# Scatter of a step's last turn behind the second layer, maximum parts ahead of the first turn's scatter, early fetches one unit later: a fused attention and routed feed-forward kernel on one Trainium2 core

## The chip, the cores and the metric

One core of a Trainium2 chip runs the whole program in one launch. The metric is device time in microseconds (us). The core has TensorE (PE, matrix products), VectorE (DVE), ScalarE (ACT), GpSimd (POOL) and SyncE (SP, which only issues transfers here). Each engine works through its own queue in order and waits on semaphores. GpSimd issues indirect transfers: gathers and scatters of rows by a list of indices.

## What is computed

`x` has 16 batches of 256 tokens with 128 features. The rows are normalised. From them come two things: causal attention with 16 heads of 8 features (low-rank corrections to the weights, a linear position bias), and a feed-forward network of 8 experts, of which each token uses one.

```python
xn = _layernorm(x, axis=-1)
s = _L0_attn_ref(xn, ...)            # softmax(q k^T / sqrt(8) + alibi + mask) v, then Wp
# experts:
indices = jnp.argmax(softmax(xn @ Wr + br), axis=-1)
for i in range(8):
    mask = (indices == i)[..., None]
    h = relu((xn * mask) @ W1[i] + b1[i])
    out = out + (h @ W2[i] + b2[i])
g = _silu(out)
return x + s * g
```

## The kernel before

**Steps and turns.** The attention runs as `NB` = 16 steps, one batch each. A step `i` has `NG` = 6 turns `g` = 0 to 5 (`GROUPS`, line 81). A turn has two units of scores (the last has one); a unit is a set of head pairs of one block row. For a unit TensorE makes the scores of step `i` (lines 1246 and 1254) and, beside them, the scores of step `i + 2` from which only the row maxima are taken (lines 1226 and 1234, read by VectorE at line 807). ScalarE turns the scores into probabilities (line 746). The products with the values come in bursts (line 1298): the last burst of a step stands in turn 0 of the next.

**Maximum parts.** The row maxima of a batch are split by GpSimd into three bf16 parts, five small instructions (`max_parts`, lines 552 to 560). TensorE transposes them at turn 2 (`turn_max`, line 1309), ScalarE copies them out (line 650), and SyncE stores them into the stack of queries at turn 3 (`load_max_rows`, line 416). The scores of the next step wait for that store. GpSimd makes the parts of batch `i + 1` at turn 0 of step `i`.

**Experts.** The tokens are sorted by expert into `SLOT_TILES` = 39 tiles of 128 rows. GpSimd gathers the rows of a tile from DRAM (`fetch_rows`, line 519), TensorE transposes four tiles at a time (line 1340), applies the first layer (`hidden`, line 1348) and the second (`output`, line 1356). VectorE applies relu (line 1030) and moves the result into one of three buffers `y_slot` (`keep_y`, line 1036); GpSimd scatters it to the rows of the tokens in DRAM (`scatter_y`, line 533). `TURNS` gives each tile a turn: tiles 0 to 3 stand at turns 21 to 24, counted over all steps, the others at `g` = 2, 3, 5 and 0. At a tile's turn TensorE makes first its first layer, then the second layer of the tile before it. The scatter of tile `t` stands at `SCATTER_TURNS[t]`: turns 23, 24, then every turn with `g` = 2, 3, 5 or 0 to turn 78, which holds two. There tile `t + 2` has its first layer. Fetches stand at `FETCH_AT`: tiles 0 to 11 one a turn from (2, 4) to (4, 3), the others at `g` = 4, 5, 1 and 2.

**Order on GpSimd.** The loop at lines 583 to 600 writes it out by hand: in each turn the fetches, at `g` = 3 the third part of a batch four steps ahead (line 506), the scatters, at `g` = 0 the maximum parts. In front of a fetch or a scatter stands a wait for a bank that TensorE filled, which sets when in the turn GpSimd issues it.

**SyncE.** At turn 0 it stores zeros and the first parts of queries and keys of batch `i + 3` (lines 405, 411, 373, 379), at turn 1 the second parts. From turn 80, that is (13, 2), it loads the experts' rows back in eight transfers (`load_y`, line 449); the first waits until all scatters have landed.

**End.** ScalarE applies tanh (line 710), VectorE multiplies and adds (lines 1042, 1048, 1053), SyncE stores.

Of the kernel before, what the change touches and what calls it, by code (L numbers as in the profile page):

```python
# [33 lines left out]
NB, T, D = 16, 256, 128  # L34
# [63 lines left out]
TILES_AT = {place: (t,) for t, place in enumerate(PLACES)}  # L98
# [107 lines left out]
def program(nc, x, w_dense, lora, br, b1, w_experts, const_f32, const_bf16, const_rows, zero_rows, out):  # L206
# [14 lines left out]
    with ctx:  # L221
# [129 lines left out]
        def wait_vec_full(eng, *key):  # L351
            k, use = VEC[key]
            eng.wait_ge(vec_full[k], use + 1)
            return vec_bank[k], vec_empty[k]

        def wait_act_full(eng, *key):
            k, use = ACTS[key]
            eng.wait_ge(act_full[k], use + 1)
            return act_bank[k], act_empty[k]

        def wait_vec_emptied(eng, *key):
            k, use = VEC[key]
            eng.wait_ge(vec_empty[k], use + 1)
# [130 lines left out]
        def _(pool):  # L494
# [7 lines left out]
            def third_part(b):  # L502
                r = b % PART_BUFS
                wait(pool, f"q3_out{r}", 16 * COPIES[2] * (b // PART_BUFS))
                pool.wait_ge(S["part2_done"], b + 1)
                pool.tensor_tensor(parts[:, r, 2], rem[:, b % 2], parts[:, r, 1], ALU.subtract).then_inc(S["part3_done"], 1)  # L506
# [4 lines left out]
            def fetch_rows(t):  # L511

                q = t // 4
                if t == 0:
                    pool.wait_ge(S["rows_done"], 1)
                    pool.wait_ge(S["rows_kept"], 16 * 4)
                if q >= 2:
                    wait_act_full(pool, "rows", q - 2)
                pool.indirect_dma_start(xs_slot[:, q % 2, t % 4, :], None, xn_dram[:, :],  # L519
                                        bass.IndirectOffsetOnAxis(from_row[:, t:t + 1], axis=0)).then_inc(S[f"xs_in{t % 8}"], 16)  # L520

            def tile_numbers():

                pool.wait_ge(S["tile_place_done"], 1)
                pool.tensor_tensor(tile_hot[:, :, 1, :], tile_hot[:, :, 1, :], tile_ids.unsqueeze(2).to_broadcast([P, NT, SLOT_ROWS]),
                                   ALU.mult).then_inc(S["tile_hot_done"], 1)

            def scatter_y(t):

                wait_vec_emptied(pool, "y", t)  # L530
                if t == 0:
                    pool.wait_ge(S["tokens_done"], 1)
                pool.indirect_dma_start(y_dram[:, :], bass.IndirectOffsetOnAxis(token_of[:, t:t + 1], axis=0),  # L533
                                        y_slot[:, t % 3, :], None).then_inc(S[f"y_out{t % 3}"], 16)
# [11 lines left out]
            def max_parts(b):  # L546

                r = b % 2
                for u in range(NU):
                    wait_vec_emptied(pool, "max", b, u)  # L550
                wait_act_full(pool, "nmax", b - 2)
                pool.tensor_scalar(nmax[r][:, :, 0, :], row_max[r][:, :, :], -1.0, None, ALU.mult).then_inc(S["nmax1"], 1)
                pool.wait_ge(S["nmax1"], b + 1)
                pool.tensor_tensor(nmax_rem[:, :, :], row_max[r][:, :, :], nmax[r][:, :, 0, :], ALU.add).then_inc(S["nmax_r"], 1)
                pool.wait_ge(S["nmax_r"], b + 1)
                pool.tensor_scalar(nmax[r][:, :, 1, :], nmax_rem[:, :, :], -1.0, None, ALU.mult).then_inc(S["nmax2"], 1)
                pool.wait_ge(S["nmax2"], b + 1)
                pool.tensor_tensor(nmax_rem2[:, :, :], nmax_rem[:, :, :], nmax[r][:, :, 1, :], ALU.add).then_inc(S["nmax_r2"], 1)
                pool.wait_ge(S["nmax_r2"], b - 1)
                pool.tensor_scalar(nmax[r][:, :, 2, :], nmax_rem2[:, :, :], -1.0, None, ALU.mult).then_inc(S["nmax3"], 1)  # L560
# [22 lines left out]
            for i in range(NB):  # L583
                for g, units in enumerate(GROUPS):
                    for t in FETCH_AT.get((i, g), ()):
                        wait_act_full(pool, "scores", i, units[0])
                        fetch_rows(t)
                    if g == PROJECT + 2 and i + AHEAD < NB:
                        third_part(i + AHEAD)
                    for t in range(SLOT_TILES):  # L590
                        if SCATTER_TURNS[t] == i * NG + g:
                            if g in (0, 3):
                                wait_act_full(pool, "scores", i, units[1])
                            elif TILES_AT[i, g][0] < SLOT_TILES:
                                wait_vec_full(pool, "hidden", TILES_AT[i, g][0])
                            scatter_y(t)
                    if g == 0 and 0 < i < NB - 1:
                        max_parts(i + 1)
                    if (i, g) == TILE_HOT_AT:
                        tile_numbers()  # L600

# [940 lines left out]
```

## Time and profile before

| | us |
|---|---|
| median of 3 runs | 317.42 |
| lowest and highest | 315.58, 317.52 |
| the profiled execution | 316.19 |
| its span, first to last instruction | 314.3 |
| busy in it: TensorE | 291.0 |
| VectorE | 214.8 |
| ScalarE | 206.6 |
| GpSimd | 132.8 |

The granted clock of TensorE is 0.986 of full on average. GpSimd issues 39 gathers and 39 scatters. The profiled execution is 1.23 us below the median of the runs. The chain of work that ended last goes for 76% of the span through TensorE. The release "issue" in a row means that the engine waited for nothing that the profile shows.

### The profile page before, as it was taken

To read this page: it belongs to the slowest core of one execution; us is meant where nothing else is said; L and a number is where in the kernel's file an instruction comes from. 1 tells how busy PE (TensorE), PEld (TensorE's weight loads), DVE (VectorE), ACT (ScalarE), POOL (GpSimd) and SP (SyncE) were. 2 spreads that over 40 slices of the span, in tenths; PEclk is the share of its full clock that TensorE was granted. 3 is DMA by queue.
4 is the path that set the end of the run, shared out by engine and by line. 5 is a ranking of instruction groups with operands and counts; after the bars stand their busy time and mean duration, and the time that the engine had idled before them with its cause. 6 is when DMAs were issued, how large, how long until landed. Compare 5 with 4: busy or idle time off the path is not lost.

```text
span 314.3 us, 13158 instructions
## 1 busy us (share of the span) xinstructions
PE 291.0 (93%) x5330; PEld 221.9 (71%) x5330; DVE 214.8 (68%) x480; ACT 206.6 (66%) x379; POOL 132.8 (42%) x210
## 2 busy tenths in 40 slices
PE   8899989898979899999999999999999998989893
PEld 3467468575657778878787787878878786867652
DVE  4788996899955475665657566575756656574893
ACT  2343265645568487777787777787777866669981
POOL 3065271122354646655645565564656422241000
PEclk9999999999979999999999999999999999999996
DMA  4799499643141311414223142231414222008432
GB/s 136 211 235 206 123 292 339 162 134 93 28 118 48 108 52 49 116 49 116 57 64 86 50 114 58 80 83 37 116 51 103 67 53 79 20 29 240 141 99 71
DMA packets 46811, 33.89 MB, mean 108 GB/s; under 512 B 5048, under 2 KB 44216, under 8 KB 46624
## 3 DMA queue, kind: packets, MB, share of 16 engines
q1 hardware_dynamic: 42520, 26.80, 31.8%
q0 software_dynamic: 2496, 5.12, 6.1%
q10 hardware_dynamic: 1736, 1.14, 1.5%
q8 instruction: 43, 0.70, 1.0%
q14 instruction: 16, 0.13, 0.1%
HBM read 13.17 MB, written 6.75 MB: 63 GB/s over the span
## 4 chain that ended last, share of the span: by engine, by line
PE 76%; DVE 11%; issue 4%; ACT 4%; DMA 2%; SPq 1%; POOL 0%; ACTq 0%; DVEq 0%; POOLq 0%
PE bank L1348 13%; PE bank L1298 12%; PE bank L1246 11%; PE bank L1356 11%; PE bank L1254 5%; DVE row_max L807 4%; PE bank L1159 4%; PE bank L1332 3%; PE bank L1166 3%; PE bank L1318 2%; DVE w_slots L972 2%; ACT probs L746 2%; PE bank L1226 2%; PE bank L1175 2%; PE bank L1340 2%
## 5 line engine op out<-in xcount | busy, mean ns | idle before, releaser
L807 DVE TENSOR_REDUCE row_max<-bank 128x2 f32<-128x512 f32 (+3 forms) x176 | 106.9, 637 | 31.8 <-PE bank L1234 29.1
L746 ACT ACTIVATE probs<-bank 128x512 f32<-128x512 f32 (+1 forms) x176 | 90.1, 560 | 33.9 <-PE bank L1254 31.7
L1246 PE MATMUL bank<-qk_stack 64*64 64x64 bf16 (+3 forms) x1024 | 60.9, 236 | 3.4 <-DVE row_max L807 1.5
L1226 PE MATMUL bank<-qk_stack 64*64 64x64 bf16 (+3 forms) x1024 | 61.4, 236 | 0.8 <-DMA qk_stack<-parts 0.5
L519 POOL DMA_INDIRECT xs_slot<-normalised_rows,from_row x39 | 38.4, 985 | 47.1 <-PE bank L1254 41.4
L533 POOL DMA_INDIRECT expert_rows<-y_slot,token_of x39 | 38.6, 991 | 46.1 <-PE bank L1348 32.8
L1030 DVE TENSOR_TENSOR hT<-bank,w_slots 128x512 f32<-128x512 f32 x39 | 27.0, 692 | 35.5 <-PE bank L1348 34.8
L722 ACT ACTIVATE w_slots<-w_all 128x1156 f32 x39 | 45.6, 1169 | 4.5 <-issue 3.2
L1246 PEld LDWEIGHTS bank<-qk_stack 64*64 64x64 bf16 x1024 | 34.1, 107 | 20.0 <-issue 8.5
L1298 PE MATMUL bank<-probs,v_diag 128*32 128x64 f32 (+3 forms) x1024 | 45.9, 304 | 1.2 <-issue 1.0
L1348 PE MATMUL bank<-xsT_slot,w_slots 128*128 128x128 f32 x312 | 45.3, 285 | 1.5 <-issue 1.5
L1254 PE MATMUL bank<-cb 64*64 64x128 bf16 (+2 forms) x352 | 43.3, 241 | 0.0
L1234 PE MATMUL bank<-cb 64*64 64x128 bf16 (+2 forms) x352 | 43.2, 241 | 0.0
L1356 PE MATMUL bank<-w_slots,hT 128*128 128x128 f32 x312 | 42.0, 276 | 0.2
L1348 PEld LDWEIGHTS bank<-xsT_slot,w_slots 128*128 128x128 f32 x312 | 38.1, 191 | 3.9 <-issue 1.8
L1356 PEld LDWEIGHTS bank<-w_slots,hT 128*128 128x128 f32 x312 | 38.2, 192 | 1.5 <-issue 1.4
L1226 PEld LDWEIGHTS bank<-qk_stack 64*64 64x64 bf16 x1024 | 33.7, 107 | 5.9 <-issue 4.7
L1298 PEld LDWEIGHTS bank<-probs,v_diag 128*32 128x32 f32 x1024 | 25.1, 109 | 12.4 <-issue 1.7
L506 POOL TENSOR_TENSOR parts<-rem,parts 128x512 bf16<-128x512 f32 x15 | 17.5, 1164 | 20.1 <-ACT parts L634 19.9
L1133 PE MATMUL bank<-zeros 128*128 128x512 bf16 x60 | 18.8, 420 | 2.3 <-POOL zeros L496 1.0
L641 ACT ACTIVATE v_diag<-bank 64x256 f32<-64x256 f32 x32 | 12.1, 379 | 12.9 <-PE bank L1166 11.8
L1254 PEld LDWEIGHTS bank<-cb 64*64 64x64 bf16 x352 | 19.8, 108 | 0.0
(134 smaller groups left out, 379.0 us busy)
## 6 DMA issues: line engine op xcount, KB each, us to landing
qk_stack<-parts SPq DMA_DIRECT2D x120, 64.0 KB
qk_stack<-parts SPq DMA_DIRECT2D x32, 128.0 KB
w_all<-w_experts SPq DMA_DIRECT2D x8, 512.0 KB, 5.9
normalised_rows<-xn_all SPq DMA_DIRECT2D x4, 512.0 KB, 6.9
xn_all<-expert_rows SPq DMA_DIRECT2D x8, 256.0 KB, 4.9
out<-xn_all SPq DMA_DIRECT2D x7, 256.0 KB, 2.5
x_all<-x SPq DMA_DIRECT2D x3, 512.0 KB, 5.2
xs_slot<-normalised_rows,from_row POOLq DMA_INDIRECT x39
```

What stands on the lines that cost most here:

```text
L519: pool.indirect_dma_start(xs_slot[:, q % 2, t % 4, :], None, xn_dram[:, :], bass.IndirectOffsetOnAxis(from_row[:, t:t + 1], axis=0)).then_ ...
L533: pool.indirect_dma_start(y_dram[:, :], bass.IndirectOffsetOnAxis(token_of[:, t:t + 1], axis=0), y_slot[:, t % 3, :], None).then_inc(S[f"y ...
L722: act.activation(w_slot[t % 3], w_all[:, bass.ds(e, 1), :].rearrange("p o f -> p (o f)"), ACT.Copy).then_inc(S["w_done"], 1)
L746: act.activation(probs[:, m % PROBS, 0:w], bank[:, 0:w], ACT.Exp).then_inc(emptied, 1)
L807: dve.tensor_reduce(row_max[b % 2][:, n, pairs[0]:pairs[-1] + 1], bank[:, 0:ln_u * len(pairs)].rearrange("p (c k) -> p c k", k=ln_u), AX.X ...
L1226: pe.matmul(bank[to, c * ln_u:(c + 1) * ln_u], q[rows, p, n * BLK:(n + 1) * BLK], k[rows, p, 0:(n + 1) * BLK], start=(c == 0), stop=False, ...
L1234: last = pe.matmul(bank[to, 0:ln_u * len(pairs)].rearrange("p (c k) -> p c k", k=ln_u)[:, :, n * BLK:], ident_b[rows, rows], mask_qk[rows] ...
L1246: pe.matmul(bank[rows, c * ln_u:(c + 1) * ln_u], k[rows, p, kb * BLK:(kb + 1) * BLK], q[rows, p, kb * BLK:], start=(c == 0), stop=False, s ...
L1254: last = pe.matmul(bank[rows, 0:ln_u * len(pairs)].rearrange("p (c k) -> p c k", k=ln_u)[:, :, 0:BLK], ident_b[rows, rows], mask_kq[rows]. ...
L1298: last = pe.matmul(pv_bank[32 * j:32 * j + 32, half * T + kb * BLK:(half + 1) * T], v_diag[b % 2][:, kb, p, :], probs[:, (b * NU + w) % PR ...
L1348: last = pe.matmul(bank[:, c * P:(c + 1) * P], w_slot[t % 3][:, c * P:(c + 1) * P], xsT_slot[:, t // 4 % 2, t % 4, :], start=(c == 0), sto ...
L1356: last = pe.matmul(bank[:, 0:D], hT[:, t % 2, c, :], w_slot[t % 3][:, W2 + c * D:W2 + (c + 1) * D], start=(c == 0), stop=(c == NC_H - 1))
```

## The change

In GpSimd's loop, and nowhere else:

- A fetch at `g` = 0 (tiles 2 and 8) waits for the scores of the turn's second unit instead of the first.
- `max_parts` stands ahead of the turn's scatters instead of behind them.
- A scatter at `g` = 5 waits until the second layer of the tile before the turn's tile is in its bank, instead of the first layer of the turn's tile.

```diff
             for i in range(NB):
                 for g, units in enumerate(GROUPS):
                     for t in FETCH_AT.get((i, g), ()):
-                        wait_act_full(pool, "scores", i, units[0])
+                        wait_act_full(pool, "scores", i, units[-1] if g == 0 else units[0])
                         fetch_rows(t)
+                    if g == 0 and 0 < i < NB - 1:
+                        max_parts(i + 1)
                     if g == PROJECT + 2 and i + AHEAD < NB:
                         third_part(i + AHEAD)
                     for t in range(SLOT_TILES):
                         if SCATTER_TURNS[t] == i * NG + g:
                             if g in (0, 3):
                                 wait_act_full(pool, "scores", i, units[1])
+                            elif g == 5:
+                                wait_vec_full(pool, "y", TILES_AT[i, g][0] - 1)
                             elif TILES_AT[i, g][0] < SLOT_TILES:
                                 wait_vec_full(pool, "hidden", TILES_AT[i, g][0])
                             scatter_y(t)
-                    if g == 0 and 0 < i < NB - 1:
-                        max_parts(i + 1)
```

## Rows read from the trace of the kernel before

**Rows 1.** The page: busy time, share of the span and instructions of each engine.

```profile
PE 291.0 (93%) x5330; PEld 221.9 (71%) x5330; DVE 214.8 (68%) x480; ACT 206.6 (66%) x379; POOL 132.8 (42%) x210
```

**Rows 2.** Stretches of steps 7 and 11: length, busy per engine, clock, transfers.

```profile
149.70:168.95 19.25, 18.49 (x343) 15.13 (x343) 11.92 (x23) 14.44 (x26) 10.48 (x15) 1.00 0.28 74
...
224.74:243.21 18.47, 18.06 (x343) 14.98 (x343) 11.82 (x23) 14.16 (x26) 10.56 (x15) 1.00 0.31 73
```

**Rows 3.** Chain of waits, first turns of steps 4, 7 and 10: start, us, what.

```profile
106.92 0.75 PE bank L1348 x5
...
111.74 0.87 PE bank L1159 x4
...
164.91 0.53 PE bank L1348 x3
...
168.95 0.86 PE bank L1159 x4
...
221.50 1.09 PE bank L1348 x8
...
224.74 0.86 PE bank L1159 x4
```

**Rows 4.** Timeline of TensorE: start, us, instruction, idle before and its releaser.

```profile
108.92 0.27 PE L1348 MATMUL bank<-xsT_slot,w_slots 128*128 128x128 f32 x1 [0.58 <-issue]
...
166.20 0.59 PE L1348 MATMUL bank<-xsT_slot,w_slots 128*128 128x128 f32 x3 [0.33 <-issue]
```

**Rows 5.** Timeline of GpSimd from step 6's last turn into step 7.

```profile
162.80 1.00 POOL L533 DMA_INDIRECT expert_rows<-y_slot,token_of  x1 [0.53 <-PE bank L1348]
164.73 0.98 POOL L533 DMA_INDIRECT expert_rows<-y_slot,token_of  x1 [0.94 <-PE bank L1254]
165.74 0.33 POOL L552 TENSOR_SCALAR nmax<-row_max 128x32 bf16<-128x32 f32 x1
...
167.18 0.29 POOL L560 TENSOR_SCALAR nmax<-nmax_rem 128x32 bf16<-128x32 f32 x1
168.36 1.05 POOL L519 DMA_INDIRECT xs_slot<-normalised_rows,from_row  x1 [0.89 <-PE bank L1254]
```

**Rows 6.** Chain of waits, the second layer in that last turn.

```profile
162.51 0.89 PE bank L1356 x8
```

**Rows 7.** Timeline of GpSimd from step 3's last turn into step 4.

```profile
104.64 1.00 POOL L533 DMA_INDIRECT expert_rows<-y_slot,token_of  x1 [0.30 <-issue]
106.59 0.98 POOL L519 DMA_INDIRECT xs_slot<-normalised_rows,from_row  x1 [0.95 <-PE bank L1254]
107.87 1.00 POOL L533 DMA_INDIRECT expert_rows<-y_slot,token_of  x1 [0.30 <-issue]
```

**Rows 8.** Timeline from step 12's last turn to the start of step 14.

```profile
274.34 0.96 POOL L533 DMA_INDIRECT expert_rows<-y_slot,token_of  x1 [6.10 <-PE bank L1348]
...
278.60 0.96 POOL L533 DMA_INDIRECT expert_rows<-y_slot,token_of  x1 [1.61 <-DVE y_slot L1036]
...
281.02 0.29 POOL L560 TENSOR_SCALAR nmax<-nmax_rem 128x32 bf16<-128x32 f32 x1
281.36 0.29 PE L1309 MATMUL bank<-cb,nmax 128*32 128x64 bf16 x8 [1.02 <-POOL nmax L560]
...
282.14 0.38 SPq L449 DMA_DIRECT2D xn_all<-expert_rows  x1
282.56 0.62 SPq L416 DMA_DIRECT2D qk_stack<-nmaxT  x1
...
286.04 0.41 PE L1246 MATMUL bank<-qk_stack 64*64 64x256 bf16 x4
```

**Rows 9.** The page, transfer queues: packets, MB, share of 16 engines' span.

```profile
q8 instruction: 43, 0.70, 1.0%
```

**Rows 10.** Transfers by line: count, KB each, median us to landing.

```profile
out<-xn_all SPq DMA_DIRECT2D x2, 128.0 KB, 1.8
```

## The prediction

> **What bounds the kernel now.** I read the page's busy shares first. TensorE is busy 291.0 of 314.3 us and the next engine 214.8 [rows 1], so a change that only moves GpSimd's work can give back no more than TensorE's idle time, some 23 us with start and end, or stretched time of the matmuls themselves. Then the stretches by step: a step of the middle takes 18.4 to 19.3 us, with TensorE busy 18.06 of 18.47 in a short one and 18.49 of 19.25 in a long one [rows 2]. So the steps are bound by TensorE, yet equal work differs by 0.8 us. To find where, I read the chain of waits at the first turn of a step, from the start of a tile's first layer (line 1348) to the start of the projection (line 1159). That stretch holds the same instructions in every step. It lasts 3.24 us in step 10 (221.50 to 224.74; steps 5 and 11 come within 0.04 of it), but 4.04 in step 7 (164.91 to 168.95) and 4.82 in step 4 (106.92 to 111.74) [rows 3]. The same two rows of step 6 give 3.77, those of steps 8 and 9 give 3.50 each. Over 3.24 that is 0.53 + 0.80 + 0.26 + 0.26 = 1.85 us for steps 6 to 9, and 1.58 us for step 4. The timeline shows what the excess is: TensorE stops in the middle of the eight matmuls of one tile, where the kernel has no wait, with "issue" as the releaser [rows 4]. A last place stands apart: in step 13 TensorE waits 1.02 us for the maximum parts of GpSimd (line 560) [rows 8]. In steps 4 to 12 GpSimd releases TensorE nowhere.
>
> **The change, part by part.**
>
> **1. Scatter at g == 5 waits for `y` instead of `hidden`** (10 places, (3, 5) to (12, 5)). It adds and removes no instruction. In step 7 the scatter starts at 162.80 and the second layer at 162.51, where the first ended, so it follows its releaser by some 0.3 us [rows 5, 6]. The second layer takes 0.89 in the chain [rows 6], so it ends at 163.40 and the scatter starts at about 163.7 instead of 162.80: 0.9 us later, ending 164.7. Behind it on GpSimd stands what the first turn of the next step brings. The buffer it empties is wanted two tiles later (`keep_y` of tile t + 3, at g == 2, about 173.5), ten microseconds on, so by itself this costs nothing; if that cover were gone, each microsecond of delay would come back on VectorE, then on the bank that it empties.
>
> **2. Maximum parts ahead of the scatter at g == 0.** The five parts run from 165.74 to 167.47, 1.73 us [rows 5]. Started when part 1's scatter ends, they run from about 164.7 to 166.45. Their inputs are there: the step's last maxima come at the end of the turn before, and the parts never waited for them here. The scatter behind them waits for the second unit's scores as before, which have been full since before 164.73, and runs from 166.6 to 167.6 instead of 164.73 to 165.71. It is the queue item that gets later, by 1.9 us; its buffer is wanted at g == 3, eight microseconds on. Next in GpSimd's queue is the fetch at (i, 1), at 168.36 [rows 5]: still free to start on time, but now only a fraction of a microsecond behind a scatter instead of behind the parts. The fetched rows are wanted many turns later. Priced as waits, parts 1 and 2 are worth 0 in steps 5 to 12.
>
> **3. Early fetches.** Only the fetches at g == 0 are touched, tiles 2 and 8. That of tile 2 stands in a queue that runs behind after the row numbers come late, and both units of its turn are scored before the transfer ahead of it ends, so I give it 0. That of tile 8 starts at 106.59 and moves by the length of one unit, some 0.3 us. More matters the scatter behind it: 107.87, 0.30 us after the fetch ended [rows 7]. After the change the 1.73 us of parts stand between these two, so it starts near 110; nothing is taken off the path by that unless the stop of part 4 goes with it.
>
> **4. What the stops cost.** No row prices a stop against the place of an indirect transfer, so I bound it from both sides. The stops in the middle of a tile's or a burst's matmuls in steps 3 to 9 all lie in the first turn, in which SyncE's six to seven stores to the stacks meet GpSimd's transfers; TensorE's 0.58 us stop of step 4 ends at 108.92, right behind the end of the second of two transfers standing 0.30 us apart (107.87 + 1.00) [rows 4, 7]. In step 7 the 0.33 us stop comes just after the one at 164.73 [rows 4, 5]. With the scatter of the first turn moved 2 us back and the fetch-scatter pair of step 4 opened, step 4 may lose its 1.58 us and steps 6 to 9 their 1.85 us: that is the gain's end, -3.4. The other end is nothing, or the stops of the rival below. For step 4, whose pair is really taken apart, I take -0.9, a little over half; for steps 6 to 9, where the same transfers still fall into the same crowd, -0.5, about a quarter, since three steps with the same order (5, 10, 11) show none [rows 3].
>
> The chip's instruction stream crosses the same engines: queue 8 moved 43 packets and 0.70 MB in the run, some 16 KB each [rows 9]. The Trainium skill (Runtime: NRT & Kernel Launch, Instruction fetch mechanics) says that instructions are refilled in 16 KiB blocks and that this is hidden, because the sequencer dispatches slower than the refill. The packet size agrees; the stops inside one tile's matmuls [rows 4] speak against "hidden", but no row names their cause. By that rule the stops would have nothing to do with transfers and part 4 would be 0 instead of -1.4; this is the second rival.
>
> **5. Step 13.** The scatter of (12, 5) starts at 274.34 and would start at about 275.2 (0.9 us later, as in part 1), ending 276.2. The parts then run from 276.2 to 277.95, 3.4 us ahead of their end at 281.31 now, and the 1.02 us wait at 281.36 goes [rows 8]. What is late next? Both scatters of (13, 0) come behind the parts: the first at about 278.1, the last, 0.96 + 0.30 us on, at 279.4 instead of 278.60: 0.8 us later. SyncE's first load of the expert rows (line 449) waits for it: now 282.14, which would be 282.9. Behind that in the same queue stands the load of the maximum rows (line 416), now 282.56, then 283.4, and TensorE needs it for step 14, now at 286.04, wanted at 285.02 if the 1.02 us is kept [rows 8]. Its time to landing is at least about the 1.8 us of the output's 128 KB stores [rows 10], and at most 3.48 (286.04 less 282.56), since TensorE does not wait there now. So TensorE would wait between 0.2 and 1.8 us, and this step is worth from -0.8 to +0.8. I take 2.3 us, nearer to the lone small store than to a landing in a crowd: it lands at 285.7, and -0.4 is left. That the row is fetched a step ahead in all other steps is why this matters only here.
>
> **Sum:** -0.9 - 0.5 - 0.4 = -1.8 us against the profiled execution, whose 316.19 us are the span of 314.3 and 1.9 around it: 314.4. The median of the three runs, 317.42, lies 1.2 above that execution (their lowest, 315.58, lies 0.6 below it), so against the median I say 315.6.
>
> **Rivals.**
>
> **All stops go** (chance 0.2). What ends them is the distance between GpSimd's transfers and the thick of the stores. For it: every stop lies there. Against it: steps 5, 10 and 11. It would give 3.4 us and another 0.4 to 0.8 from step 13, so -4.0: 313.4.
>
> **Nothing of the stops changes** (0.24). SyncE's stores alone, or the refill by itself, make them, and the scatter is one of eight or so transfers of the turn. The Trainium skill (Trainium Kernel Development and Optimization, Key Constraints) puts SP's, ACT's and POOL's transfers on the same 16 engines, where they interleave; by it a scatter moved by 2 us inside the same crowd is no relief. Only step 13 is left, -0.4: 317.0.
>
> **A new pair in every step** (0.11, the slower side). The scatter of (i, 0) ends at 167.6 and the fetch of (i, 1) follows: 0.3 to 0.7 us between two indirect transfers in steps 4 to 11, eight times, where 1.73 us of parts stood before. If closeness of two such transfers is what stops TensorE, at 0.5 to 0.8 us each (step 6's and 7's excess), eight pairs cost 4.0 to 6.4, less what step 4 gets back: about +3.5, 321. Against it: the scatter at 104.64 stands 0.30 us behind a fetch too, with no stop beside it [rows 7], and by 168 us SyncE has issued all stores of the turn. It decides from some six pairs that stop for 0.5 us.
>
> **The wait at g == 5 does not bite** because GpSimd arrives late anyway: here it is idle 0.53 us ahead of 162.80 [rows 5], so the new wait does move it; I fold the few hundredths of chance for it into the second rival.
>
> **How the numbers follow.** The forecast case has 0.45, the rivals 0.20, 0.24 and 0.11. Own range of the forecast case: 314.3 to 317.2, from the ends of step 13 and half the ends of part 4. The whole range goes down to the middle of the first rival and up past the second with the runs' own spread: 313.2 to 318.4, leaving out the slower rival and the far end of the first. 1% is 3.2 us, about what can be told from no change. Faster by more: the first rival's 0.20 less a little, and the lower edge of the forecast's, 0.27. Slower by more: 0.11 of the last rival, rounded to 0.12. Within: 0.61.
>
> **What would show it.** Part 1: the scatter of a g == 5 turn starts 0.8 to 1.0 us later within its step, behind line 1356. Part 2: the five parts end near the place where they began, the scatter behind them, no `keep_y` idle. Part 4: the stretch from line 1348 to line 1159 at the first turn is near 3.3 us in step 4 and in steps 6 to 9; if it stays at 3.5 to 4.0 there, I was wrong to credit it, and if it grows in steps 5, 10 and 11 the pairs are guilty. Part 5: line 1309 of step 13 no longer waits for line 560, while line 449 starts 0.8 us later and TensorE may show a wait on a transfer at the start of step 14. The prediction falls if the total moves by over 3 us either way.

## The result and the profile after

The changed kernel took 317.57 us (median of 22 runs) against 315.81 us (22 runs) of the kernel before in the same comparison. The ratio is 1.0055, 95% interval 1.0036 to 1.0075: a small loss, about 1.7 us, where I had forecast a small gain. Later sets of runs, told of below, gave two kinds of answer: some in which the kernel before takes about 305 us and the change gains 0.2 to 0.3%, and some in which it takes about 316. The sets at about 305 ran on chips 12, 0, 0 and 4, the later set at about 316 on chip 8; for the first comparison no chip is on record. Whether the difference goes with the chip or with something else about a set is not known: no chip gave both answers.

The page after has the same busy time of TensorE in a longer span (compare [rows 1]):

```profile
span 315.6 us, 13158 instructions
...
PE 291.1 (92%) x5330; PEld 221.9 (70%) x5330; DVE 216.2 (68%) x480; ACT 206.6 (65%) x379; POOL 133.0 (42%) x210
```

Step 11 as a stretch, from turn 1 to turn 1 (columns as in [rows 2]); it takes 19.17 us where the kernel before had 18.47 in [rows 2]. This stretch goes from line 1320 to line 1320, the start of turn 1, that of [rows 2] from line 1159 to line 1159; both span one whole step:

```profile
224.68:243.85 19.17, 18.29 (x350) 15.15 (x343) 11.93 (x22) 14.23 (x24) 10.46 (x14) 1.00 0.30 72
```

Lines of the changed kernel from 600 on are two higher: 1350 is the first layer, 1300 the burst of products with the values. The chain of waits in the first turn of step 10 shows where the time went. It answers to the last two rows of [rows 3]. In the kernel before the burst ahead of them took 0.82 us:

```profile
220.68 0.82 PE bank L1298 x32
```

In the changed kernel:

```profile
220.80 0.68 PE bank L1300 x22
221.48 0.21 issue
221.69 0.40 PE bank L1300 x9
222.09 1.09 PE bank L1350 x8
223.18 0.89 PE bank L1358 x8
...
224.75 0.59 PE bank L1320 x4
225.34 0.86 PE bank L1161 x4
```

From line 1350 to line 1161 it is now 3.25 us, clean, as it was at best before. The eight long matmuls of a tile no longer stop. The burst of 32 short matmuls ahead of them does: 0.68 + 0.21 + 0.40 = 1.29 us. Of the 0.47 us more only 0.21 shows as idle. The timeline of step 8 (the same in steps 5 to 13) sets it beside GpSimd:

```profile
182.23 0.99 POOL L533 DMA_INDIRECT expert_rows<-y_slot,token_of  x1 [1.42 <-PE bank L1358]
182.55 0.75 PE L1300 MATMUL bank<-probs,v_diag 128*32 128x128 f32 x23
183.26 0.33 POOL L552 TENSOR_SCALAR nmax<-row_max 128x32 bf16<-128x32 f32 x1
183.56 0.40 PE L1300 MATMUL bank<-probs,v_diag 128*32 128x64 f32 x9 [0.26 <-issue]
```

The scatter's preparation on GpSimd ends at 183.22; TensorE is idle from 183.30. In all nine steps 5 to 13 the distance from that end to the stop lies between 0.07 and 0.12 us. The new wait ties the scatter to the end of the second layer, so its end falls into the burst each time. I call that end the launch of the transfer.

Step 13 answers to [rows 8]:

```profile
280.01 1.03 POOL L533 DMA_INDIRECT expert_rows<-y_slot,token_of  x1 [0.39 <-issue]
281.35 0.97 POOL L533 DMA_INDIRECT expert_rows<-y_slot,token_of  x1 [0.31 <-issue]
281.49 2.12 PE L1300 MATMUL bank<-probs,v_diag 128*32 128x256 f32 x16
283.27 0.30 PE L1311 MATMUL bank<-cb,nmax 128*32 128x64 bf16 x8
283.66 0.38 SPq L449 DMA_DIRECT2D xn_all<-expert_rows  x1
284.21 0.62 SPq L416 DMA_DIRECT2D qk_stack<-nmaxT  x1
```

Line 1311 waits no more for the parts. But the two scatters that now follow the parts, 0.31 us apart, run over the burst of 16 at (13, 1), which takes 2.12 us. In the kernel before it took 1.07:

```profile
279.27 1.07 PE L1298 MATMUL bank<-probs,v_diag 128*32 128x256 f32 x16
```

The 1.02 us won is spent again. One launch alone did not stretch this burst before: the last scatter of [rows 8] ends at 279.56, 0.3 us into it, and TensorE does not stop. The same holds for the bursts of 16 matmuls at turn 1 of steps 3 and 4 of the changed kernel, with launches at 93.65 and 112.16. So a launch inside a burst is not enough by itself for a stop; what sets the burst of 32 apart is not known.

### The profile page after: what moved, and what is told of

The parts are those of the page before. It is cut to its first block, busy times and chain, and to the rows that moved or that the text cites. A ratio compares the mean times of both kernels' runs of the same rounds, so it can differ in the third digit from the quotient of the medians.

```text
span 315.6 us, 13158 instructions
## 1 busy us (share of the span) xinstructions
PE 291.1 (92%) x5330; PEld 221.9 (70%) x5330; DVE 216.2 (68%) x480; ACT 206.6 (65%) x379; POOL 133.0 (42%) x210
## 4 chain that ended last, share of the span: by engine, by line
PE 75%; DVE 12%; ACT 4%; issue 4%; DMA 2%; SPq 1%; DVEq 1%; ACTq 0%
PE bank L1350 13%; PE bank L1300 12%; PE bank L1248 12%; PE bank L1358 11%; PE bank L1256 5%; DVE row_max L809 5%; PE bank L1334 3%; PE bank L1161 3%; PE bank L1168 3%; PE bank L1320 2%; DVE w_slots L974 2%; PE bank L1228 2%; ACT probs L748 2%; PE bank L1177 2%; PE bank L1342 2%
## 5 line engine op out<-in xcount | busy, mean ns | idle before, releaser
L809 DVE TENSOR_REDUCE row_max<-bank 128x2 f32<-128x512 f32 (+3 forms) x176 | 108.0, 637 | 38.5 <-PE bank L1236 33.5
L748 ACT ACTIVATE probs<-bank 128x512 f32<-128x512 f32 (+1 forms) x176 | 91.1, 560 | 44.4 <-PE bank L1256 39.0
L1300 PE MATMUL bank<-probs,v_diag 128*32 128x64 f32 (+3 forms) x1024 | 49.3, 305 | 3.1 <-issue 2.8
L1248 PEld LDWEIGHTS bank<-qk_stack 64*64 64x64 bf16 x1024 | 33.9, 106 | 20.7 <-issue 8.7
L1350 PE MATMUL bank<-xsT_slot,w_slots 128*128 128x128 f32 x312 | 44.3, 285 | 0.0
L1358 PE MATMUL bank<-w_slots,hT 128*128 128x128 f32 x312 | 41.3, 275 | 0.0
L1300 PEld LDWEIGHTS bank<-probs,v_diag 128*32 128x32 f32 x1024 | 26.8, 109 | 15.8 <-issue 5.7
L1228 PEld LDWEIGHTS bank<-qk_stack 64*64 64x64 bf16 x1024 | 33.2, 106 | 6.2 <-issue 5.0
L506 POOL TENSOR_TENSOR parts<-rem,parts 128x512 bf16<-128x512 f32 x15 | 17.5, 1166 | 20.2 <-ACT parts L636 19.9
L1256 PEld LDWEIGHTS bank<-cb 64*64 64x64 bf16 x352 | 19.7, 107 | 0.0
L1236 PEld LDWEIGHTS bank<-cb 64*64 64x64 bf16 x352 | 19.6, 107 | 0.0
```

The lines of the kernel that those rows point to most:

```text
L748: act.activation(probs[:, m % PROBS, 0:w], bank[:, 0:w], ACT.Exp).then_inc(emptied, 1)
L809: dve.tensor_reduce(row_max[b % 2][:, n, pairs[0]:pairs[-1] + 1], bank[:, 0:ln_u * len(pairs)].rearrange("p (c k) -> p c k", k=ln_u), AX.X ...
L1228: pe.matmul(bank[to, c * ln_u:(c + 1) * ln_u], q[rows, p, n * BLK:(n + 1) * BLK], k[rows, p, 0:(n + 1) * BLK], start=(c == 0), stop=False, ...
L1236: last = pe.matmul(bank[to, 0:ln_u * len(pairs)].rearrange("p (c k) -> p c k", k=ln_u)[:, :, n * BLK:], ident_b[rows, rows], mask_qk[rows] ...
L1248: pe.matmul(bank[rows, c * ln_u:(c + 1) * ln_u], k[rows, p, kb * BLK:(kb + 1) * BLK], q[rows, p, kb * BLK:], start=(c == 0), stop=False, s ...
L1256: last = pe.matmul(bank[rows, 0:ln_u * len(pairs)].rearrange("p (c k) -> p c k", k=ln_u)[:, :, 0:BLK], ident_b[rows, rows], mask_kq[rows]. ...
```

## The experiments

Each experiment was timed against the kernel before on the same chip. Ratios have their 95% interval.

### Parts alone

The first set: the new wait alone; the maximum parts alone; the change without the new wait; and the change with a later wait.

```diff
# the wait alone: the kernel before with
+                            elif g == 5:
+                                wait_vec_full(pool, "y", TILES_AT[i, g][0] - 1)
# the parts alone: max_parts(i + 1) moved ahead of the scatters
# the later wait: the changed kernel with
-                                wait_vec_full(pool, "y", TILES_AT[i, g][0] - 1)
+                                pool.wait_ge(S["pv_ps"], (i + 1) * NPV)
```

> The kernel before with the new wait of the scatters at g = 5 alone. Theory A (every pause of TensorE begins some 0.1 us after GpSimd has finished preparing an indirect transfer, and the new wait puts that moment into the burst of short matmuls at line 1298): a stop of about 0.2 us in that burst in each of the ten steps, the burst 1.3 us long instead of 0.82, so the whole slowdown of the change or more is here, ratio to before 1.006 to 1.012 (the early gain of step 4 and of part 2 missing). Theory B (the new neighbourhood of the first turn's scatter and the fetch behind it makes the loss): no change here, 0.998 to 1.002.

> The kernel before with the maximum parts ahead of the first turn's scatter, nothing else. Theory A: the scatter of g = 5 keeps its place, so the burst at line 1298 stays at 0.82 us; the first turn's scatter now finishes beside the second layer, the scores of the next turn or the transposition at line 1318, and the stops of steps 4 and 6 to 9 in line 1348 go: ratio 0.985 to 0.997, with line 1309 of step 13 no longer waiting. Theory B: the loss is here, ratio 1.003 to 1.010.

> The changed kernel with the wait at g = 5 put back (maximum parts first, early fetches one unit later). Theory A: like maximum parts first alone, 0.985 to 0.997 of before, that is 1 to 2% below the changed kernel. Theory B: 1.003 to 1.010 of before, the changed kernel's own time.

> The changed kernel with the scatters of g = 5 made to wait still longer, until the burst at line 1298 of the next step's first turn is done. Theory A: what hurts is the moment, not the lateness; the end of the preparation leaves the burst and falls about 1.3 us behind it, into the long matmuls of lines 1350 and 1358: burst back to 0.82 us, ratio to before 0.990 to 1.001. Theory B (a later scatter pushes the whole queue of GpSimd and its transfers into the next turn): worse than the changed kernel, 1.008 or more.

The kernel before took 305.2 us here, with the instructions as long as in the first trace. The wait alone: 0.9994 (0.9975 to 1.0013). The parts alone: 0.9970 (0.9939 to 1.0002). The change without the wait: 0.9983 (0.9959 to 1.0008). The later wait: 1.0060 (1.0037 to 1.0082). Theory A's loss for the wait did not come, for there was no stop in any burst. So the set could not judge it. The later wait lost by something else: in step 13 everything behind the burst is late, and the maximum rows with it.

```profile
277.29 0.41 PE L1248 MATMUL bank<-qk_stack 64*64 64x256 bf16 x4 [1.87 <-DMA qk_stack<-nmaxT]
```

### The change itself in such a set

Unaltered kernels, and the wait alone again.

> The changed kernel unaltered, beside the kernel before on the same chip. In the first comparison the kernel before took 315.8 us and TensorE stopped for 0.2 to 0.6 us about 0.1 us after indirect transfers were prepared; in the single-part runs it took 305.2 and no such stop was seen. Theory A (the loss is made of these stops): where there are none the change is not slower, ratio 0.996 to 1.001; where they are back, 1.003 to 1.008. Theory B (the loss comes from the order of the waits and is there on any chip): 1.004 to 1.008 in either case.

> The kernel before unaltered, one look, for its trace on the chip of this set. Theory A: if it takes about 305 us, steps 6 to 12 are 18.1 us each with no stop in lines 1298 or 1348; if it takes about 316, the stops of the first trace are there again.

> The new wait at g = 5 alone once more, on the chip of this set. Theory A: where the kernel before takes about 316 us, a stop in the burst at line 1298 of each step and a ratio of 1.004 to 1.012; where it takes about 305, 0.998 to 1.002 as before. Theory B: the same ratio on both.

The kernel before: 305.4 us median. The changed kernel: 0.9973 (0.9961 to 0.9986), the wait alone 1.0011 (0.9996 to 1.0027). So the change is faster where the stops are missing, and its steps 6 to 11 are 18.06 or 18.07 us from turn 1 to turn 1, as those of the kernel before. In the changed kernel the scatter of step 8 runs from 176.07 to 177.06, inside the burst, and the chain has the burst whole:

```profile
176.07 0.99 POOL L533 DMA_INDIRECT expert_rows<-y_slot,token_of  x1 [1.42 <-PE bank L1358]
```

```profile
176.46 0.80 PE bank L1300 x32
177.26 0.31 PE bank L1350
```

The 0.27% is step 13. The kernel before waits there as in [rows 8], the changed kernel waits for the maximum rows a little later instead:

```profile
271.00 0.29 PE L1309 MATMUL bank<-cb,nmax 128*32 128x64 bf16 x7 [1.02 <-POOL nmax L560]
```

```profile
275.16 0.38 PE L1248 MATMUL bank<-qk_stack 64*64 64x256 bf16 x3 [0.45 <-DMA qk_stack<-nmaxT]
```

From turn 1 of step 13 to turn 1 of step 14 it is 9.51 us instead of 10.23: 0.72 less.

### The dose, and the parts where launches pause TensorE

This set had the kernel before at 316.5 us. First an extra gather of 128 rows at each g = 5, ten in all, whose data is not used; the same with a plain transfer; the kernel before with the maximum parts first in step 13 only and the first load of expert rows behind the maximum rows; and the parts alone.

```diff
# the dose: the kernel before with, behind the scatter of g == 5,
+                                wait_vec_full(pool, "y", TILES_AT[i, g][0] - 1)
+                                wait(pool, "probe_in", 16 * (i - 3))
+                                pool.indirect_dma_start(probe[:, :], None, xn_dram[:, :], ...from_row[:, 0:1]...)
# or, plain:
+                                pool.dma_start(probe[:, :], xn_dram[0:P, :])
```

> The kernel before with one more gather of 128 rows into a spare tile at each g = 5, launched when the changed kernel launches its scatter there; its data is not used. Theory A on a chip where launches pause TensorE (kernel before about 316): a stop of 0.2 to 0.3 us in the burst at line 1298 of every step 4 to 13, 3 to 6 us more, ratio 1.010 to 1.020. On a chip without pauses (about 305): 0.999 to 1.002, for transfers and their preparation are hidden. Theory C (what pauses is the instruction refill behind a crowd of transfers): stops not bound to the place, in some steps only.

> As the gather before, but a plain transfer of the same 64 KB issued by GpSimd, its data not used either. If the pause belongs to indirect transfers alone: ratio of the gather kernel not reached, 0.999 to 1.003 on both kinds of chip. If it belongs to any transfer that GpSimd prepares: like the gather.

> The kernel before with maximum parts first in step 13 alone, and SyncE's first load of expert rows put behind the load of the maximum rows; scatters and fetches elsewhere as before. Both theories: the 1.02 us wait at line 1309 goes, and the wait on the maximum rows at the start of step 14 that the changed kernel had instead (0.45 us) does not come: 0.9 to 1.3 us less than before, ratio 0.996 to 0.998, on a chip with pauses and on one without.

> Maximum parts first alone once more. On a chip without pauses 0.996 to 0.998 as measured. On a chip with pauses, theory A: the burst at line 1298 stays whole, so at least as good as on the other, 0.990 to 0.999; theory B: the scatter of the first turn and the fetch behind it make the loss, 1.003 to 1.008.

The dose: 1.0426 (1.0383 to 1.0470), 329.06 us, or 1.26 us for each gather, two to four times what I expected. Here line 1304 is the burst, 602 the extra gather; scatter and gather end at 188.20 and 189.46:

```profile
187.20 1.00 POOL L535 DMA_INDIRECT expert_rows<-y_slot,token_of  x1 [0.53 <-PE bank L1354]
188.50 0.96 POOL L602 DMA_INDIRECT probe<-normalised_rows,from_row  x1 [0.31 <-issue]
```

```profile
189.40 0.34 PE L1304 MATMUL bank<-probs,v_diag 128*32 128x64 f32 x4 [0.32 <-issue]
190.36 0.43 PE L1304 MATMUL bank<-probs,v_diag 128*32 128x64 f32 x12 [0.62 <-issue]
```

TensorE stops twice in the burst: at 189.09, 0.9 us behind the end of the scatter and while the gather is still being prepared, and at 189.74, 0.28 us behind the gather's end. The first keeps no such short distance to an end as the nine of the changed kernel do. In seven of the eight steps 5 to 12 it lies over packets of the scatter itself, which in step 8 begin to move at 188.93; in the changed kernel no packet of GpSimd's transfers is under way during any of the nine stops (in step 8 they begin at 183.89, behind it). So the dose shows what the gathers cost, and not that each stop is set by the end of a preparation; the moving data may have a share in its first stops. Its bursts in steps 4 to 13 all hold stops (in step 13, at 288, only one). Bound to the place and there in each step, they speak for the indirect transfers and against a refill of instructions that would come at other points of each step. The packets of queue 8 in the trace of the changed kernel say the same: the nearest to the nine stops begin between 2.0 us ahead of them and 2.7 us behind, and in seven of the nine stops none is under way.

The plain transfer: 1.0031 (0.9999 to 1.0063), hardly anything. Its ten preparations all end inside the burst, 0.3 to 0.6 us behind the burst's start, and none of the ten bursts has a stop. In step 8 the end is at 182.91 (TensorE's row is from the chain of waits):

```profile
182.32 0.59 POOL L602 DMA_DIRECT2D probe<-normalised_rows  x1
```

```profile
182.60 0.84 PE bank L1304 x31
```

So of the two readings, every transfer of GpSimd or the indirect ones alone, this speaks for the second. It is not clean: the plain preparation is shorter, 0.59 us against 0.96 to 1.00, and ends 0.3 us into the burst, where that of the gather ended 1.0 us after the burst had begun and that of the changed kernel's scatter 0.7 us.

The parts alone: 0.9907 (0.9882 to 0.9931), 3.4 us faster than the kernel before. The step in its chain, lines as before:

```profile
218.74 0.82 PE bank L1298 x32
219.57 1.09 PE bank L1348 x8
220.66 0.89 PE bank L1356 x8
222.22 0.59 PE bank L1318 x4
222.81 0.87 PE bank L1159 x4
```

and GpSimd beside it:

```profile
217.46 0.99 POOL L533 DMA_INDIRECT expert_rows<-y_slot,token_of  x1 [0.53 <-PE bank L1348]
218.48 0.33 POOL L552 TENSOR_SCALAR nmax<-row_max 128x32 bf16<-128x32 f32 x1
...
220.63 1.05 POOL L533 DMA_INDIRECT expert_rows<-y_slot,token_of  x1 [0.41 <-issue]
222.37 0.99 POOL L519 DMA_INDIRECT xs_slot<-normalised_rows,from_row  x1 [0.69 <-PE bank L1254]
```

The launches fall at 218.45 (in the scores, 0.3 us ahead of the burst), 221.68 (behind the second layer) and 223.36 (in the projection): none in the burst, none in the first layer. All steps from 6 to 11 last 18.44 to 18.53 us, where the kernel before had 18.44 to 19.25 in its first trace. One stop of 0.36 us in the first layer is left, in step 4. This kernel has the close pair of scatter and fetch too, 0.69 us apart where the changed kernel has 0.54, so that pair is not what costs; theory B falls.

The last-step kernel: 1.0003 (0.9973 to 1.0032), no gain where 0.2 to 0.4% was expected. Its wait at the transposition is gone as well (line 1313 there), and again two scatters, 0.30 us apart, stand beside the burst of (13, 1), lines four higher:

```profile
277.43 1.03 POOL L535 DMA_INDIRECT expert_rows<-y_slot,token_of  x1 [0.39 <-issue]
278.77 0.97 POOL L535 DMA_INDIRECT expert_rows<-y_slot,token_of  x1 [0.30 <-issue]
```

```profile
279.66 1.40 PE L1302 MATMUL bank<-probs,v_diag 128*32 128x256 f32 x13
```

Step 13 takes 9.98 us there from turn 1 to turn 1, where the kernel before had 10.25 in its first trace.

### The wait alone beside the change, twice more, and the best version

> The changed kernel in one set with its parts. Theory A on a chip with pauses (kernel before about 316): 1.003 to 1.008, the stop in the burst in every step. On a chip without (about 305): 0.996 to 0.999. Theory B, without part 1 being guilty: no link to the burst's stops.

> The new wait at g = 5 alone. Theory A on a chip with pauses: the stop in the burst of every step, and 1.005 to 1.020, since what the maximum parts in front bring (0.991 alone there) is missing. If part 1 hurts only together with part 2 (two scatters shifted by the same 1 to 2 us): 0.997 to 1.003. On a chip without pauses: 1.000.

> The changed kernel with the g = 5 scatters held until the burst is done. Theory A (place in the burst) on a chip with pauses: burst whole again at 0.80 us, 0.993 to 1.001 of before, below the changed kernel. If lateness or crowding of launches is what counts, not the burst: 1.005 to 1.015. On a chip without pauses it took 1.006, from waits of its own.

> Maximum parts first in all steps, and SyncE's first load of expert rows behind the load of the maximum rows; no new wait, no fetch change. With pauses 0.988 to 0.993, without 0.995 to 0.997: the best of all in both cases if the two gains add.

> The changed kernel beside its parts. Theory A where the kernel before takes about 316: 1.003 to 1.008 with the stop in the burst of every step; where it takes about 305: 0.996 to 0.999.

> The new wait at g = 5 alone. Theory A where the kernel before takes about 316: a stop in the burst of every step, 1.005 to 1.020. If the wait hurts only with the maximum parts moved too: 0.997 to 1.003. About 305: 1.000.

> The changed kernel with the g = 5 scatters held until the burst is done. Theory A where the kernel before takes about 316: burst whole at 0.80 us, 0.993 to 1.001. If lateness of launches counts and not the burst: 1.005 to 1.015. About 305: 1.006 to 1.008 as measured.

Both sets had the kernel before at 305.4 to 305.6 us, so neither could show the stops. The changed kernel: 0.9981 (0.9964 to 0.9998) and 0.9966 (0.9952 to 0.9979). The wait alone: 1.0007 (0.9977 to 1.0038) and 1.0015 (1.0003 to 1.0027). The later wait: 1.0078 (1.0056 to 1.0101) and 1.0056 (1.0037 to 1.0075). Maximum parts first in all steps, with the first load of expert rows put behind the maximum rows on SyncE, was the best of its set: 0.9971 (0.9959 to 0.9983).

```diff
-                    if (i, g) in LOAD_AT:
+                    if (i, g) in LOAD_AT and LOAD_AT[i, g] > 0:
+                        if LOAD_AT[i, g] == 1:
+                            load_y(0)
                         load_y(LOAD_AT[i, g])
```

Its step 13 takes 9.02 us from turn 1 to turn 1, 1.2 less than before; the parts alone in their first set, without that order, had 9.02 too. So the order of the loads gave nothing that was measured. The parts alone are the version to take: 0.991 in the one kind of set, 0.997 in the other.

## Why the prediction was wrong

**What bounds.** Right: the steps are TensorE's, and the spread between equal steps is stops in the middle of its matmuls. I even had the rows side by side in part 4, a stop of 0.58 us that ends behind a launch and one of 0.33 that begins 0.16 us behind another [rows 4, 5, 7].

**Part 1 is the step that failed.** I moved the scatter at g = 5 by 0.9 us (measured: it starts 1.42 us after the fetch ahead of it instead of 0.53, 0.89 later) and priced that at nothing in steps 5 to 12, because I asked only who waits for the buffer. I did not carry the launch that comes 1 us behind the start against TensorE's own sequence. 163.7 + 1.0 is 164.7, and the burst of step 7 began at 164.08 and lasted 0.83. The price was 0.45 to 0.60 us in each burst of steps 6 to 12, by the chain of waits. A second cost stood behind it: the wait for ScalarE ahead of the values' projection at turn 3 (line 1166, now 1168) grew from about 0.40 us to between 0.47 and 0.71 us per step; it was 4.1 us instead of 2.8 over steps 5 to 11. For that second one I have only the trace; which launch makes ScalarE late was not isolated.

**Part 4** was half right. The stops in the first layer did go, all 1.85 us of steps 6 to 9, not the quarter that I took. Others came in the burst. The two go apart: the kernel with the parts alone lost the first in steps 5 to 12 and did not gain the second. From turn 1 of step 5 to turn 1 of step 12 the sum was: bursts +3.5, first layer -1.85, turn 3 +1.3, together +3.0; measured 133.81 us against 130.71, so +3.1. Ahead of that the changed kernel had gained 1.00 us: its turn 1 of step 5 begins at 129.11 instead of 130.11. Step 4 took 18.75 us from turn 1 to turn 1 instead of 20.91, which is 2.2 less and not the 0.9 I had put there, but step 5 took 0.77 more, and 0.42 had been lost ahead of turn 1 of step 2. Behind turn 1 of step 12 the changed kernel is 0.84 us shorter, of which 0.76 stands behind the last matmuls of line 1320; I have no cause for that. -1.00 + 3.10 - 0.84 is the +1.26 of the two spans. Not all of step 4's gain is the change: the kernel before had a granted clock of 0.78 on average from 88 to 92 us and 0.80 from 92 to 96, the changed kernel 1.00 in both, and so had the kernel before in its later trace.

**Part 5** was right in its mechanism and nearly in size where launches do not pause TensorE: 1.02 us gone, then a wait of 0.45 for the maximum rows behind the load of expert rows, net -0.72 against my -0.4. I had added 0.8 us of delay to line 449; in that set it was 0.14 (271.77 against 271.63), although the last scatter started 1.23 us later (269.47 against 268.24). The load waits for the landing of the scatters, and the later start did not carry through to it; why it did not was not looked into. Where launches pause, the same failing as in part 1 took it back: I placed the two scatters at 278.1 and 279.4 and did not look at the burst beside them.

**The rivals.** "A new pair in every step" had the sign but not the mechanism: the kernel with the parts alone has the same pair and is the fastest of its set. "All stops go" is near to what happened without the new wait: none is left in the bursts and first layers of steps 5 to 12, one of 0.36 us in step 4. I had worked out 4.0 us for it; the ratio 0.9907 is 3.4. The Trainium skill's rule that the refill of instructions is hidden (Runtime: NRT & Kernel Launch, Instruction fetch mechanics) is not contradicted: the stops keep a fixed distance to launches, 0.07 to 0.12 us in nine steps, and in seven of the nine no refill is under way.

**What is shown and what is open.** Shown: that gathers launched inside the burst cost 1.26 us each when ten are added, and plain transfers launched there next to nothing; that the change puts a launch there in each step, with a stop behind it; that without the new wait, the parts moved, the time falls to 0.9907. Not shown by a run: the new wait alone where launches pause TensorE, for the four sets that held it were all of the other kind, and the later wait there. That part 1 is the cause of the 0.55% thus rests on the traces, the dose, and the difference between 1.0055 and 0.9907, which are from two comparisons. Those two kernels differ also by part 3, two fetches in steps 3 and 4, and the kernel that sets the wait apart from it was timed only where the kernel before takes 305 us. Open too is why some sets show no pauses, why a single launch left the bursts of 16 alone, and what in the launch of an indirect transfer holds the engines, which the plain one lacks.

## What to carry to other kernels

A wait that shifts an indirect transfer moves two things: when its buffer comes free, and when it is launched, one microsecond behind its start. Lay the launch beside the matmuls of TensorE: here the burst of 32 short ones stopped at each of nine launches, while launches beside the scores and the projection left the steps even at 18.44 to 18.53 us. And compare a change of this size on more than one set of runs: the same edit was +0.55% in one and -0.2 to -0.3% in three.

## What the runs showed of the hardware

- Where the kernel before takes 316 us, TensorE stopped for 0.2 to 0.6 us. In the changed kernel the stops of steps 5 to 13 began some 0.1 us behind the launch of an indirect transfer; in the dose they did not keep that distance, and two launches 1.26 us apart, one ahead of the burst and one in it, went with 0.3 and 0.6 us of idle. ScalarE and VectorE show waits put down to "remote" in these traces (in the kernel before, ScalarE at line 736: 7.6 us in six waits, some beside stops of TensorE and some not).
- Where it takes 305 us, the same instructions are as long (burst of 32: 0.80 us) and the steps 18.06 us, with no such stop and no "remote" wait. Of the difference of 11 us, 10.5 arises between turn 1 of step 2 and turn 1 of step 13, 204.79 us against 194.29. Stops, and a wait for ScalarE at turn 3 of 0.4 us in place of 0.05, are part of it; the rest was not taken apart.
- The store of the maximum rows, 32 KB, issued at 272.19 right behind a load of 256 KB, was waited for until 275.16: about 3 us, in the upper half of the 1.8 to 3.48 that I had bounded, where I had taken 2.3.
